# Eight experts on 1024 tokens: dense over all tokens, against rows routed into 23 tiles by expert

## What is computed

```python
def _L0_ffn_ref(x, Wg, bg, W1, b1, W2, b2):        # x (4, 1024, 128), E = 8, K = 2
    gate_probs = softmax(x @ Wg + bg)
    _, top_idx = top_k(gate_probs, 2)
    expert_mask = one_hot(top_idx, 8).sum(-2)
    selected = gate_probs * expert_mask
    selected = selected / (selected.sum(-1, keepdims=True) + 1e-08)
    h = gelu(einsum('bsf,efh->bseh', x, W1) + b1)   # W1 (8, 128, 512)
    expert_out = einsum('bseh,ehf->bsef', h, W2) + b2   # W2 (8, 512, 128)
    return einsum('bsef,bse->bsf', expert_out, selected)
```

## Time and profile before

| what | us |
| --- | --- |
| runs | 2635.10, 2643.84, 2647.67 |
| median of the runs | 2643.84 |
| profiled execution | 2645.18 |
| its span, first to last instruction | 2643.1 |
| TensorE busy in it | 2017.8 |
| front 0 alone, to the end of x3 | 453.8 |
| of it the experts, from the end of x1 to the add of b2 | 127.8 |
| back 3 alone | 301.3 |

### The profile page before, as it was taken

How to read it: one execution, slowest core, us unless ns; L and a number is a source line. 1 busy time by engine, 2 the same in 40 slices (tenths; PEclk the granted TensorE clock), 3 DMA queues, 4 the chain that set the end, 5 groups by cost and what they waited for, 6 DMA issues and landing times.

```text
span 2643.1 us, 38819 instructions
## 1 busy us (share of the span) xinstructions
PE 2017.8 (76%) x14843; PEld 1256.7 (48%) x14843; DVE 1314.4 (50%) x2660; ACT 1241.3 (47%) x2610; POOL 592.8 (22%) x505
## 2 busy tenths in 40 slices
PE   2865986489867987679868976788757999758776
PEld 1123664244344755333545754442345666535454
DVE  4134225654366145445654157734665545467574
ACT  2642421376644331667543333566645565235453
POOL 0420000263311001235400011433510221024231
PEclk8776995698978986888888987888978999778998
DMA  3000000000000100000000000000100110000000
GB/s 112 1 1 1 25 25 1 10 16 10 25 5 17 41 13 5 5 13 17 25 14 16 33 9 9 13 5 17 33 5 5 33 33 17 0 20 21 13 17 13
DMA packets 32059, 45.50 MB, mean 17 GB/s; under 512 B 7824, under 2 KB 18948, under 8 KB 31748
## 3 DMA queue, kind: packets, MB, share of 16 engines
q1 hardware_dynamic: 31875, 43.01, 6.0%
HBM read 24.12 MB, written 2.10 MB: 10 GB/s over the span
## 4 chain that ended last, share of the span: by engine, by line
PE 53%; DVE 25%; ACT 10%; issue 7%; POOL 4%; SPq 1%; DVEq 0%; DMA 0%; ACTq 0%; POOLq 0%
PE PH L933 8%; PE PD L893 8%; PE PH L716 5%; PE PB L1082 4%; PE PB L1102 4%; PE PB L1018 3%; ACT back_arena L1345 2%; PE PD L760 2%; PE PB L1039 2%; PE PB L1138 2%; POOL front_arena L1936 2%; ACT front_arena L1213 2%; DVE back_arena L1818 2%; DVE back_arena L1817 1%; PE PB L1029 1%
## 5 line engine op out<-in xcount | busy, mean ns | idle before, releaser
L1973 POOL TENSOR_TENSOR back_arena<-back_arena 128x512 f32<-128x512 f32 x128 | 165.4, 1294 | 1052.3 <-DVE back_arena L1818 1052.2
L1213 ACT ACTIVATE front_arena<-PD 128x1024 f32<-128x1024 f32 (+3 forms) x384 | 303.3, 817 | 160.7 <-PE PD L760 159.0
L1302 ACT ACTIVATE front_arena<-PD,b 128x512 f32<-128x512 f32 x256 | 161.6, 683 | 260.6 <-PE PD L893 260.4
L933 PEld LDWEIGHTS PH<-W,front_arena 128*128 128x128 f32 x2048 | 248.2, 192 | 65.6 <-issue 34.1
L1936 POOL TENSOR_TENSOR front_arena<-front_arena,tri 128x256 f32<-128x256 f32 x256 | 201.1, 798 | 322.4 <-ACT front_arena L1213 321.6
L933 PE MATMUL PH<-W,front_arena 128*128 128x128 f32 x2048 | 255.3, 276 | 7.6 <-DVE R L1664 6.7
L1082 PE MATMUL PB<-wqkv,hT 128*128 128x512 f32 x384 | 233.1, 696 | 32.5 <-DVE back_arena L1818 12.7
L893 PE MATMUL PD<-xT,W 128*128 128x512 f32 x512 | 246.4, 605 | 1.2 <-ACT xT L1196 1.2
L716 PE MATMUL PH<-front_arena 128*32 128x512 f32 (+3 forms) x1536 | 189.4, 569 | 66.2 <-POOL front_arena L1936 41.5
L1825 DVE TENSOR_REDUCE fnm<-PB 128x4 f32<-128x512 f32 x128 | 88.3, 691 | 303.6 <-PE PB L1102 302.0
L1345 ACT ACTIVATE back_arena<-PB,fnm 128x128 f32<-128x128 f32 x512 | 180.9, 371 | 111.0 <-DVE fnm L1825 110.8
(11 more groups left out here) (241 smaller groups left out, 3398.0 us busy)
## 6 DMA issues: line engine op xcount, KB each, us to landing
W<-in_W SPq DMA_DIRECT2D x32, 512.0 KB, 3.4
back_arena<-back_arena SPq DMA_DIRECT2D x128, 128.0 KB, 2.3
X<-in_L_attn_hidden SPq DMA_DIRECT2D x64, 32.0 KB, 1.8
out_y<-Nb SPq DMA_DIRECT2D x64, 32.0 KB, 1.6
wqkv<-in_L_ffn_wqkv SPq DMA_DIRECT2D x1, 1536.0 KB
back_arena<-in_c_xpos SPq DMA_DIRECT2D x1, 1024.0 KB
back_arena<-in_L_ffn_w SPq DMA_DIRECT2D x1, 682.0 KB
wo<-in_L_ffn_wo SPq DMA_DIRECT2D x1, 512.0 KB
```

The lines of the kernel that those rows point to most:

```text
L933: ins = pe.matmul(p[:, 128 * t:128 * t + 128], hv[:, c, 128 * t:128 * t + 128], W12[e % WRING][:, HF + 128 * c:HF + 128 * c + 128], start= ...
L1213: act.activation(pb[:, :, 0:n], p[:, :, 0:n], ACT.Exp, scale=INV_SQRT_HD).then_inc(freed(b, "S", half, g, kc, jp), 1)
L1973: pool.tensor_tensor(T1[k % 2][:, hs, :], T1[k % 2][:, hs, :], T2[:, hs, :], ALU.add).then_inc(sg("rot"), 1)
```

## The change

The experts are no longer applied to all tokens. Each token's row is copied once for each of its two experts into a table of 23 tiles of 128 rows in DRAM, sorted by expert, each expert's part padded to whole tiles. Always all 23 tiles are worked on. By steps:

- **Counts** (`count_ahead`, label rk). After the second choice, VectorE signals the sum of both choices (`chosen`). TensorE makes eight products with a matrix of ones (the number of tokens of each expert), one with the triangle `tri` (tokens of the same expert ahead in the tile) and seven that add the tiles before.
- **b2**: GT, the b2 product and its add, now to x itself, stand ahead of the slots.
- **Slots** (`tokens_to_slots`). VectorE makes from the counts the first row of each expert, from that the row of each token for either choice (`rows`, 11 steps), then the expert of each tile (`expert`, three steps) and the token's two gate values (`share`, two).
- **Scatter** (labels sc 0 to 7). GpSimd issues 16 indirect DMAs, one per tile of tokens and choice, 128 rows of 512 bytes each, from XX into x_rows in DRAM.
- **Weights.** SyncE reads the expert of a tile from SBUF into a register (`value_load`) and loads that expert's weights, with b1 packed behind them (526 KB), into a ring of WRING = 6. The first six are loaded as soon as `expert` is there; those of pair i+3 wait for the second layer of pair i.
- **Rows back in.** When all 16 scatters have landed, three DMAs load the 23 tiles into `xs` (rows on the partition), and TensorE turns them in groups of 8, 8 and 7 (`rows_turned`, label sT), with ScalarE's copies to xsT.
- **Products.** `first_products` and `second_products` go over 12 pairs of tiles, with 128 columns per product. The first layer of pair i+1 is issued ahead of the second of pair i. ScalarE's gelus have 128 elements, as the bias is now that of the tile's expert. VectorE copies the result over the pair's rows in `xs`, and SyncE stores them to y_rows every second pair.
- **Gather** (labels ga 0 to 7). When all stores have landed, GpSimd issues 16 indirect DMAs that bring each token's two rows back, and VectorE adds them to R with the two shares, 16 scaled adds in two halves (cmb).

At the start, x_rows is cleared by one DMA on SyncE ahead of the first weights, from a tile of zeros that GpSimd sets (ZEROS is now 7). The order table is made by the same `order` from a new list of front steps, in which each pair of scatters and of gathers has an assumed duration of 3 and no time on an engine. The diff is cut, and dedented by 12 columns.

```diff
-WRING = 2
+WRING = 6
+SLOTS = 2 * NT + E - 1
+PAIRS = (SLOTS + 1) // 2
+ROW = HF + HC * 128 + HC
...
+    for t in range(NT):
+        add(("sc", t), 0, 3)
+    add(("sT", 0), 1, 2, 1)
+    for i in range(PAIRS):
...
+        add(("h", i), 2, 2, 2.9)
+        if i:
+            add(("eo", i - 1), 2, 2, 0, 0.4)
...
+    for t in range(NT):
+        add(("ga", t), 0, 3)
...
-    def load_expert(e):
-        sp.dma_start(W12[e % WRING][:, :], A["W12"][e]).then_inc(sg(f"w_in{e % WRING}"), 16)
+    def load_experts(i):
+        for j in range(2 * i, min(2 * i + 2, SLOTS)):
+            e = sp.value_load(expert[0:1, j:j + 1], min_val=0, max_val=E - 1)
+            sp.dma_start(W12[j % WRING], A["W12"][bass.ds(e, 1)].rearrange("o p n -> (o p) n")).then_inc(sg(f"w_in{j % WRING}"), 16)
...
+                sp.wait_ge(sg("zeros"), ZEROS)
+                sp.dma_start(x_rows.rearrange("(p t) d -> p t d", t=SLOTS),
+                             Nb[:, 0:1, :].to_broadcast([128, SLOTS, 128])).then_inc(sg("x_zero"), 16)
...
+            yield front_at(b, "slots")
+            sp.wait_ge(sg("experts"), b + 1)
+            for i in range(WRING // 2):
+                load_experts(i)
+            yield front_at(b, "sT", 0)
+            sp.wait_ge(sg("x_rows"), 256 * (b + 1))
+            for i in range(3):
+                n = min(8, SLOTS - 8 * i)
+                sp.dma_start(xs[:, 8 * i:8 * i + n, :], x_slots[:, 8 * i:8 * i + n, :]).then_inc(sg(f"xs_in{i}"), 16)
+            for i in range(PAIRS):
+                yield front_at(b, "eo", i)
+                if i + WRING // 2 < PAIRS:
+                    read(sp, b, "eo", i)
+                    load_experts(i + WRING // 2)
+                if i % 2:
+                    is_free(sp, b, "eo", i)
+                    n = min(4, SLOTS - 2 * i + 2)
+                    sp.dma_start(y_slots[:, 2 * i - 2:2 * i - 2 + n, :], xs[:, 2 * i - 2:2 * i - 2 + n, :]).then_inc(sg("y_rows"), 16)
...
+    def count_ahead(b):
+
+        pe.wait_ge(sg("chosen"), b + 1)
+        p = fill(pe, b, "rk")
+        both = gtmp[3].rearrange("p t e -> p (t e)")
+        for t in range(NT):
+            pe.matmul(p[:, E * NT:E * NT + E], ones_m, both[:, E * t:E * t + E], start=(t == 0), stop=(t == NT - 1))
+        pe.matmul(p[:, 0:NT * E], tri[:, :], both, start=True, stop=False, skip_group_check=True)
+        for t in range(NT - 1):
+            later = p[:, E * (t + 1):E * NT].rearrange("p (t e) -> p t e", e=E)
+            ins = pe.matmul(later, ones_m, both[:, E * t:E * t + E].unsqueeze(1).to_broadcast([128, NT - 1 - t, E]),
+                            start=False, stop=(t == NT - 2), skip_group_check=True)
+        ins.then_inc(filled(b, "rk"), 1)
+
+    def rows_turned(b, i):
+        yield front_at(b, "sT", i)
+        pe.wait_ge(sg(f"xs_in{i}"), 16 * (b + 1))
+        p = fill(pe, b, "sT", i)
+        for t in range(min(8, SLOTS - 8 * i)):
+            ins = pe.transpose(p[:, 128 * t:128 * t + 128], xs[:, 8 * i + t, :], ident[:, :])
+        ins.then_inc(filled(b, "sT", i), 1)
+
+    def first_products(b):
+        for i in range(PAIRS):
+            yield front_at(b, "h", i)
+            p = fill(pe, b, "h", i).rearrange("p (a c n) -> p a c n", a=2, c=HC)
+            is_free(pe, b, "sT", i // 4)
+            for j in range(2 * i, min(2 * i + 2, SLOTS)):
+                loads = (SLOTS - j % WRING + WRING - 1) // WRING
+                pe.wait_ge(sg(f"w_in{j % WRING}"), 16 * (loads * b + j // WRING + 1))
+                for c in range(HC):
+                    ins = pe.matmul(p[:, j % 2, c, :], W12[j % WRING][:, 128 * c:128 * c + 128],
+                                    xsT[j // 8 % 2][:, 128 * (j % 8):128 * (j % 8) + 128], start=True, stop=True)
+            ins.then_inc(filled(b, "h", i), 1)
+
+    def second_products(b):
+        for i in range(PAIRS):
+            yield front_at(b, "eo", i)
+            p = fill(pe, b, "eo", i)
+            is_free(pe, b, "h", i)
+            for j in range(2 * i, min(2 * i + 2, SLOTS)):
+                for c in range(HC):
+                    ins = pe.matmul(p[:, 128 * (j % 2):128 * (j % 2) + 128], hbuf[i % 2][:, j % 2, c, :],
+                                    W12[j % WRING][:, HF + 128 * c:HF + 128 * c + 128], start=(c == 0), stop=(c == HC - 1))
             ins.then_inc(filled(b, "eo", i), 1)
+
+    def experts(b):
+        yield from merged(rows_turned(b, 0), rows_turned(b, 1), rows_turned(b, 2), first_products(b), second_products(b))
...
+        for i in range(PAIRS):
+            yield front_at(b, "h", i)
...
+            if i >= 2:
+                read(act, b, "eo", i - 2)
+            p = read(act, b, "h", i).rearrange("p (a c n) -> p a c n", a=2, c=HC)
+            for j in range(2 * i, min(2 * i + 2, SLOTS)):
+                for c in range(HC):
+                    ins = act.activation(hbuf[i % 2][:, j % 2, c, :], p[:, j % 2, c, :], ACT.Gelu_apprx_tanh,
+                                         bias=W12[j % WRING][:, HF + HC * 128 + c:HF + HC * 128 + c + 1])
+            ins.then_inc(freed(b, "h", i), 1)
...
+    def tokens_to_slots(b):
...
-        frees(dve.tensor_tensor(R[:, :, :], R[:, :, :], p, ALU.add), b, "b2")
+        frees(dve.tensor_tensor(R[:, :, :], XX[b % 2][:, :, :], p, ALU.add), b, "b2")
+        yield front_at(b, "slots")
+        p = read(dve, b, "rk")
...
+        link(dve.tensor_tensor(square, p[:, NT * E:NT * E + E].unsqueeze(2).to_broadcast([128, E, E]),
+                               steps[:, 0:E].unsqueeze(1).to_broadcast([128, E, E]), ALU.is_gt))
+        link(dve.tensor_reduce(tiles[:, :], square, AX, ALU.add))
+        link(dve.tensor_tensor(square, before, tiles[:, :].unsqueeze(1).to_broadcast([128, E, E]), ALU.mult))
+        link(dve.tensor_reduce(base[:, :], square, AX, ALU.add))
+        frees(dve.tensor_tensor(ahead, p[:, 0:NT * E].rearrange("p (t e) -> p t e", t=NT),
+                                base[:, :].unsqueeze(1).to_broadcast([128, NT, E]), ALU.add), b, "rk")
+        link(dve.tensor_tensor(part, pick, ahead.unsqueeze(1).to_broadcast([128, 2, NT, E]), ALU.mult))
+        link(dve.tensor_reduce(place[:, :], part.rearrange("p k t e -> p (k t) e"), AX, ALU.add))
+        link(dve.tensor_scalar(place_i[:, :], place[:, :], -1.0, None, ALU.add))
+        dve.tensor_scalar(place[:, :], place[:, :], float(SLOTS), float(-SLOTS), ALU.mult, ALU.add)
+        link(dve.tensor_scalar(place_t[:, :], place_i[:, :], 7, None, ALU.logical_shift_right))
+        signals(dve.scalar_tensor_tensor(out=rows[:, :], in0=place_t[:, :], scalar=1.0 - 128 * SLOTS, in1=place[:, :],
+                                         op0=ALU.mult, op1=ALU.add), "rows")
...
+        signals(dve.tensor_copy(expert[:, :], of_slot[:, :]), "experts")
...
+
+    def experts(b):
+        for i in range(PAIRS):
+            n = min(2, SLOTS - 2 * i)
+            yield front_at(b, "eo", i)
+            p = read(dve, b, "eo", i)[:, 0:128 * n].rearrange("p (t n) -> p t n", t=n)
+            dve.tensor_copy(xs[:, 2 * i:2 * i + n, :], p).then_inc(freed(b, "eo", i), 1)
+        for h in range(2):
+            yield front_at(b, "cmb", h)
+            dve.wait_ge(sg(f"y_in{h}"), 128 * (b + 1))
+            for k in range(2):
+                for t in range(4 * h, 4 * h + 4):
+                    ins = dve.scalar_tensor_tensor(out=R[:, t, :], in0=Y12[:, 2 * t + k, :], scalar=share[:, k, t:t + 1],
+                                                   in1=R[:, t, :], op0=ALU.mult, op1=ALU.add)
+                link(ins)
...
+            for t in range(NT):
+                yield front_at(b, "sc", t)
+                if t == 0:
+                    if b == 0:
+                        pool.wait_ge(sg("x_zero"), 16)
+                    pool.wait_ge(sg("rows"), b + 1)
+                for k in range(2):
+                    pool.indirect_dma_start(x_rows, bass.IndirectOffsetOnAxis(ap=rows[:, NT * k + t:NT * k + t + 1], axis=0),
+                                            XX[b % 2][:, t, :], None).then_inc(sg("x_rows"), 16)
+            for t in range(NT):
+                yield front_at(b, "ga", t)
+                if t == 0:
+                    pool.wait_ge(sg("y_rows"), 16 * (PAIRS // 2) * (b + 1))
+                for k in range(2):
+                    pool.indirect_dma_start(Y12[:, 2 * t + k, :], None, y_rows,
+                                            bass.IndirectOffsetOnAxis(ap=rows[:, NT * k + t:NT * k + t + 1], axis=0)).then_inc(sg(f"y_in{t // 4}"), 16)
```

193 lines of the change are left out of this document (87 added, 106 removed).

## The result

The changed kernel takes 2694.57 us (median; 2692.11 to 2702.28), the kernel before 2642.94 in the same session. The ratio is 1.0203, with a 95% interval of 1.0171 to 1.0236: slower, by some 2%. The profiled execution took 2702.28 us with a span of 2700.2.

What follows compares the result with a forecast made beforehand. TensorE bound the expert stages, chains between engines the rest. Front 0 467.5, three stretches 1907 and the last back 301.3 give 2675.8, with span and median corrections 2677 us, 1.2% slower; own range 2657 to 2730, overall 2585 to 2775.

Steps and rivals of the forecast that it cites:

- the tail: Rest of the front behind the expert stage, images 1 to 3: a back beside it adds 27 us.
- The start: Start of the kernel: SyncE's clearing of x_rows ahead of the first weights costs 3 us.
- Front 0's chain: Image 0's expert stage, no back beside it: 137 us from x1 norm to last add, a loss of 10.7 us.
- TensorE's price ahead of the scatter: Before image 0's scatter: gate product 1.85 us, counts 3.7, turn of the gates with b2 product and add 6.0.
- The ring: Pairs of tiles: reloading the six weight tiles sets the pace, 9.05 us per two pairs, counted five times.
- With a back beside it: Images 1 to 3 from x1 on: the front's chain of 202.0 us plus 56 for the back woven in.
- The rounds' ends: Three stretches of a front with a back, summed only to the front's end: 641 us, then 633 twice, 1907.
- TensorE's work: Whole kernel: TensorE relieved of about 73 us per image, its busy time near 1730 us for 2018.
- (b): Rival for scatter and gather: the indirect DMA is dear, at 2.0 us each 2767 us; chance 0.20.
- (c): Rival beside a back: VectorE keeps GpSimd from writing, 0.9 us for each of 96 DMAs, 2763 us; chance 0.04.
- (a): Rival: the back fills the waits, 26 instead of 56 us per stretch, 2587; with a milder case 2621, together 0.25.
- (e): Rival for the whole kernel: a tie, two errors of 15 us per image cancel the loss, 2631 to 2657; chance 0.14.

Runs made afterwards that it cites:

- clear_late: The changed kernel with the clearing of x_rows issued behind all the weights instead of ahead of the first: 2653.0 us, ratio 1.003.
- ga0: The changed kernel with assumed gather-step duration 0 instead of 3 in the order table, so no back step stands among the gathers: 2692.93 us, ratio 1.0179.
- b2_late: The changed kernel with the turn of the gates, b2 product and its add moved behind the slots, beside the first scatter: 2629.64 us, ratio 0.9955.
- split: The changed kernel with each weight load in two halves, the first layer's half reloaded right after the pair's first product: 2619.57 us, ratio 0.991.

## Why the prediction came out as it did

The time lay 17.6 us above the forecast of 2677, within its range of 2657 to 2730, and on the forecast's side. The path that the forecast describes is the one that the trace shows, but the sum came out in part by luck: it lacks a loss of 37 us, and an estimate for the tail that was too large stood in its place. Without that loss the kernel would be near 2658, an estimate from clear_late's 2653.0 and the 4.7 us of the clearing. Step by step, against the profiled spans (2700.2, forecast 2675.8):

**The start.** 3 us forecast for the clearing, 4.8 measured (17.5 to 22.4), and 4.7 of it came back with clear_late.

**Front 0's chain.** 137.3 forecast, 144.1 measured. The term that was mis-sized is TensorE's price ahead of the scatter. I kept L900's 1.85 us for the gate product and twice that for the counts, without asking at which clock that row was taken. In the kernel before, TensorE also does nothing for 11 us ahead of the turn of x, and its clock is 1.2 GHz up to 269.0. It then rises, behind 3.3 us in which the first expert product kept TensorE busy throughout, and L900 runs behind that product:

```profile
265.70:269.00 3.30, 3.30 (x4) 1.51 (x5) 0.00 (x0) 1.25 (x1) 0.00 (x0) 0.50 0.00 0
270.00:274.00 4.00, 4.00 (x17) 2.36 (x17) 2.09 (x10) 3.94 (x6) 0.00 (x0) 1.00 0.00 0
```

The change takes the expert products away from this place. From the norm to the first scatter TensorE works in pieces with waits between them, 18.0 of 30.4 us, and is granted 0.50 (1.2 GHz) throughout: 3.6 us for the gate product, 7.0 for the counts, 3.8 for the b2 product against 2.05.

```profile
267.30:297.70 30.40, 18.01 (x80) 16.25 (x80) 9.61 (x40) 2.29 (x3) 0.00 (x0) 0.50 0.00 0
```

The first scatter came 30.5 us behind the norm instead of 23.0; of these 7.5, 1.7 are the gate product, 3.3 the counts and 2.1 the turn of the gates with b2 (8.1 for 6.0). The rest was close: scatter and rows 25.3 for 26.5 (the DMA 1.25 us apart for 1.3), pairs 62.2 for 59.3, the way from the last product to the last add 26.1 for 28.5.

**The ring** spaced the pairs, 10.2 us for two against 9.05 forecast. Both terms of it were off: the register step is 0.75 with its address arithmetic, not 1.0, and the landing 5.2 to 5.4, not 3.4, with the pair's first load and a store under way beside it. L627's landing in the earlier trace rows was one load's; it wasn't a price for two. The image has four such rounds where I summed five, so the pairs as a whole came only 2.9 us over.

**With a back beside it.** 202.0 + 56 = 258 forecast, 258.6 measured, 263.2 and 260.2 for images 2 and 3. The sum was right by luck, for a reason that wasn't in it. Against the front alone, piece by piece in image 1: 7.5 beside the gate (forecast 8), 11.9 in the scatter (13), nothing in the pairs (0), 15.0 in the tail (27), and 17.8 in the gather (8). Some 13 of the gather's 17.8 are the hold. In clear_late, without a hold, the gather adds 28.4 - 23.6 = 4.8 and x1 to x3 takes 244.7. So my piece for the tail was 12 too large and the hold, which I had not foreseen, filled it.

**The rounds' ends.** I let a round end with x3. It ends 6 us later, when the back before has finished (1118.1 and 1124.1): 18 us in all, the largest part of the 24.4 that were missing. The others are 1.8 at the start, 4.6 in front 0 with its tail, 8.0 in the three stretches from x1 to x3 and 1.2 in the last back, less 9.2 in the stretches up to x1. The ga0 run shows that this end is as much on the path as x3.

**TensorE's work.** 1730 forecast for its busy time, 1829.8 measured: 51.6 us less in image 0's stage where I had 73, because counts, gate and turns were costed at the full clock or left out.

**Rivals.** (b) is out by the 0.96 + 0.30 us of a DMA. The page that I had cited beside it ("DMA: Bandwidth & Descriptors" of the Trainium skill) gives about 1 us to the first byte, from the software that writes descriptors. The 0.96 us that GpSimd is busy with one lies close to it, but isn't the same thing, and the 0.30 between two is on the path too. (c): the mean of a scatter is 1036 ns for a median of 958, and 992 for 945 in the gather, 8 us in 128 DMAs, with single ones up to 1987. The rule of the Trainium skill's "SBUF — State Buffer" on VectorE keeping GpSimd from writing descriptors can be in these maxima, but it doesn't carry the time here. (a), that the back fills the waits, was half right, and the hold hid it: in clear_late image 1's stretch from x1 to x3 takes 244.7 us and image 0's, alone, 208.4, so a back costs 36 us there, between (a)'s 26 and my 56. clear_late's 2653.0 lies inside my borders of a tie (e), 2630.6 and 2657.1, and b2_late and split on the other side of them. The sign of this change hung on 37 us of hold and on two waits that are easily moved.
